# A hand-ordered two-attention kernel: paired row transfers, loads moved between queues, register loads ahead of their waits, and new weights for the planner of the step order

## The chip, the cores and the metric

The kernel runs on one core of one Trainium2 chip. The metric is the device time of one execution in microseconds (us). TensorE is called PE, VectorE DVE, ScalarE ACT, GpSimd POOL and SyncE SP. Lower is better.

## What is computed

Two transformer stages on x of shape (2, 1024, 128) in float32, each followed by a layer norm without weights:

```python
# stage 0: 8 heads of 16 features, causal, with a rank-one term per head
q, k, v = split(x @ w_qkv)
scores = q @ k.T * 0.25 + head_scales[h] * outer(q[:3] @ dirs[h], k[:3] @ dirs[h])
x = layernorm(x + softmax(causal(scores)) @ v @ w_out)
# stage 1: 16 heads of 8 features, keys and values from a latent of 64, rope
xh = rmsnorm(x); lat = layernorm(xh @ Wdkv.T) * ln_g + ln_b
q = rope(xh @ Wq.T); k = rope(lat @ Wuk.T); v = lat @ Wuv.T
x = x + softmax(causal(q @ k.T / sqrt(8))) @ v @ Wo.T
# a mixture of 4 experts, the best one alone counts for each token
e = argmax(rmsnorm(x) @ gate_w.T + gate_b)
x = layernorm(x + relu(rmsnorm(x) @ W1[e].T + b1[e]) @ W2[e].T + b2[e])
```

## The kernel before

**Groups.** Attention goes by groups of four heads of one batch: F = 0 to 3 belong to stage 0 and F = 4 to 11 to stage 1. For each group PE computes the scores once with the queries as rows, only so that DVE can take each row's maximum (steps `max`, L1370 on PE and L1887 on DVE, 20 units a group). The maxima are turned by PE (`turnmax`, L1426), split by DVE into three bf16 parts (L1747 to L1753, semaphore `np_ready`) and sent by SP into three rows of the queries' tile `qs` (step `rows`: L1094 in stage 0, L1088 in stage 1). The second pass of scores (`scores`, L1390) then subtracts them in the matmul itself; ACT takes the exponential (L1607), POOL masks the diagonal blocks (L1208), PE multiplies by the values (`pv`, L1407), ACT evacuates (L1612), PE turns and DVE divides (L1418, L1760, L1764). So a group's exponentials can't begin before its rows have landed.

**Splitting.** Queries and keys are float32 numbers split into three bf16 parts (`hi` L1632, `r1` L1901 or L1289, `mid` L1636, `lo` L1906 or L1296), in 16 blocks M of 512 tokens. Blocks 0 to 3 are batch 0 of stage 0: queries and keys of tokens 0 to 511 (M = 0, 1), then of tokens 512 to 1023 (M = 2, 3). SP stores each block to DRAM (`store`, L1076) and SP loads it again six times, once for each product of parts (`load`, L1018 in stage 0, L1010 in stage 1), into the tile of the group (`qs`, `ks`, three slots). In groups 0 to 4 each load is in two halves of 512 tokens. One exception: the keys of group 0 are loaded by POOL's queue. A load waits until its block's store has landed, and from group 3 on until the scores of the group three before are done (the slot). ACT's queue loads nothing.

**Experts.** Batch 0's tokens are sorted by expert (`places`, then eight indirect DMAs `scatter` on POOL, L1229, then `sorted` on SP), and worked on in 11 tiles: `row_turn` L1564, `row_feat`, `tile_hidden` L1574, `tile_relu` L1671, `tile_out` L1582 and L1586, `tile_sum` L1967, `tile_store` L1063, then eight indirect `collect` (L1247). Batch 1 goes densely through all experts (`hidden` L1542, `relu` L1711, `expert` L1486, `pick_up` L1981). In `tile_relu` on ACT and `tile_out` on PE the expert's number is read from SBUF into a register of the engine:

```python
pe.wait_ge(done["tile_relu"], nth("tile_relu", s, j))
wait_bank(*step)
e = pe.value_load(expert_of[0:1, j:j + 1], min_val=0, max_val=E - 1)
```

**The order.** A planner, run when the kernel is built, merges all steps into one list `SCHEDULE`. Each step has a wanted position (tables `FIRST`, `BETWEEN`, `READY`, `BY_ROWS`, `EXPERTS`, the numbers `MAX_AHEAD` and `MAX_LENGTH` for the maxima); the planner keeps model times of every engine from `COSTS` and `costs(step)`, and takes next the step whose engine would idle least, with `URGENT` as the weight of the position and `SP_IDLE`, `FEED`, `BACKLOG` as weights of idle time. Every engine, SP's queue of DMAs too, executes its steps in this order and waits on semaphores where it must. `MOST` says how many banks pairs each use of PSUM may hold.

## Time and profile before

| | us |
|---|---|
| median of 3 runs | 563.38 (559.97 to 565.47) |
| the profiled execution: its time | 565.1 |
| the profiled execution: span from first to last instruction | 563.4 |
| PE busy, PE granted clock on average | 480.2 (85%), 0.95 |
| DVE, ACT, POOL busy | 371.9 (66%), 323.6 (57%), 179.8 (32%) |

The span is the time from the first to the last instruction of the profiled execution; some 1.7 us of its time lie around it. Busy times are sums of instructions; an engine's idle time is put down to what ended it. The clock is PE's granted clock as a share of full speed (2.4 GHz); 0.50 is 1.2 GHz.

### The profile page before, as it was taken

The numbers are of one execution on the slowest core, as the hardware profiler recorded it, in microseconds if no ns is written. First come the engines' busy times: TensorE is split into PE (matmuls) and PEld (weight loads), VectorE is DVE, ScalarE is ACT, GpSimd is POOL, SyncE is SP. The second block draws the span as 40 slices with busy tenths as digits, with TensorE's granted clock in tenths as the row PEclk, the third lists the DMA queues.
The fourth block names the chain that finished last, engine by engine and source line by source line (L and its number), as shares of the span: only waits on it lengthen the run. The fifth ranks groups of instructions, "written<-read, shape, count | busy, mean of one in ns | idle before, by whom it ended". The sixth has DMA issues, their size and how long they took to land.

```text
span 563.4 us, 10237 instructions
## 1 busy us (share of the span) xinstructions
PE 480.2 (85%) x3749; PEld 223.4 (40%) x3764; DVE 371.9 (66%) x690; ACT 323.6 (57%) x488; POOL 179.8 (32%) x249
## 2 busy tenths in 40 slices
PE   5576799998899989888797998848888988999993
PEld 3242233444442333333232333312554443367762
DVE  4286977788877889688888788866356721233343
ACT  3422156576676668867685776715456677843331
POOL 9830131237554237634030222452202304601000
PEclk9977889999999999999999799976899999999998
DMA  3894030306112002012010102031000000100010
GB/s 96 214 210 132 2 96 23 94 1 243 45 56 65 25 5 83 28 52 65 17 43 9 52 3 58 6 98 45 6 12 15 8 12 20 30 1 0 20 38 20
DMA packets 31571, 28.83 MB, mean 51 GB/s; under 512 B 8017, under 2 KB 27857, under 8 KB 31250
## 3 DMA queue, kind: packets, MB, share of 16 engines
q1 hardware_dynamic: 30626, 26.34, 16.3%
q0 software_dynamic: 896, 1.84, 1.4%
q8 instruction: 31, 0.51, 0.4%
q14 instruction: 18, 0.15, 0.1%
HBM read 19.27 MB, written 9.31 MB: 51 GB/s over the span
## 4 chain that ended last, share of the span: by engine, by line
PE 58%; ACT 10%; DVE 10%; SPq 8%; issue 5%; DMA 4%; POOL 3%; ACTq 1%; another core or an unknown queue 0%; DVEq 0%; POOLq 0%
PE ps L1407 15%; PE ps L1390 10%; ACT pr L1607 7%; PE ps L1370 7%; DVE mparts L1887 6%; PE ps L1486 5%; PE ps L1542 5%; SPq L1018 4%; PE ps L1472 3%; SPq L1088 3%; DMA qs<-nparts 2%; PE ps L1466 2%; PE ps L1586 2%; PE ps L1574 2%; PE ps L1418 2%
## 5 line engine op out<-in xcount | busy, mean ns | idle before, releaser
L1887 DVE TENSOR_REDUCE mparts<-ps 128x2 f32<-128x1024 f32 (+3 forms) x240 | 260.4, 1114 | 83.0 <-PE ps L1370 78.5
L1607 ACT ACTIVATE pr<-ps 128x1024 f32<-128x1024 f32 (+1 forms) x240 | 221.2, 939 | 142.9 <-PE ps L1390 140.6
L1407 PE MATMUL ps<-pr,vs 128*32 128x512 f32 (+3 forms) x1152 | 124.4, 506 | 9.1 <-ACT pr L1607 5.7
L1390 PE MATMUL ps<-qs,ks 64*128 64x512 bf16 (+7 forms) x561 | 102.1, 339 | 21.1 <-DMA qs<-nparts 11.3
L1370 PE MATMUL ps<-ks,qs 61*128 61x512 bf16 (+7 forms) x576 | 108.7, 348 | 4.0 <-DVE mparts L1887 1.9
L1208 POOL TENSOR_SCALAR_AFFINE_SELECT pr<-pr 128x512 f32<-128x512 f32 x96 | 60.7, 635 | 156.5 <-ACT pr L1607 156.3
L1390 PEld LDWEIGHTS ps<-qs,ks 64*128 64x128 bf16 (+1 forms) x576 | 31.5, 96 | 106.7 <-issue 41.6
L1370 PEld LDWEIGHTS ps<-ks,qs 61*128 61x128 bf16 (+1 forms) x576 | 35.5, 101 | 33.3 <-ACT pr L1607 11.0
L1407 PEld LDWEIGHTS ps<-pr,vs 128*32 128x32 f32 x1152 | 23.6, 108 | 48.5 <-issue 30.1
L1711 ACT ACTIVATE work<-ps,b 128x512 f32<-128x512 f32 x32 | 21.8, 685 | 29.7 <-PE ps L1542 28.2
L1363 PE MATMUL ps<-cmask,identb 64*128 64x128 bf16 (+1 forms) x96 | 23.4, 244 | 11.8 <-DVE mparts L1887 4.8
L1486 PE MATMUL ps<-w,work 128*128 128x128 f32 x256 | 30.9, 278 | 0.0
L1486 PEld LDWEIGHTS ps<-w,work 128*128 128x128 f32 x256 | 29.3, 192 | 1.8 <-issue 1.8
L1542 PE MATMUL ps<-feat,w 128*128 128x512 f32 x64 | 29.7, 597 | 0.0
L1356 PE MATMUL ps<-cmask,identb 128*128 128x128 bf16 (+1 forms) x96 | 16.8, 260 | 8.9 <-issue 4.9
L1363 PE MATMUL ps<-cmaskx,identx 64*128 64x128 bf16 (+1 forms) x96 | 23.5, 245 | 0.0
L1981 DVE SCALAR_TENSOR_TENSOR xn<-ps,onehot,xn 128x128 f32<-128x128 f32 x24 | 6.8, 345 | 25.1 <-PE ps L1486 25.1
L1363 PEld LDWEIGHTS ps<-cmask,identb 64*128 64x128 bf16 x96 | 9.0, 94 | 36.0 <-issue 13.1
L1366 PE MATMUL ps<-cmask,identb 64*128 64x64 bf16 (+1 forms) x96 | 19.4, 202 | 0.0
L1366 PE MATMUL ps<-cmaskx,identx 64*128 64x64 bf16 (+1 forms) x96 | 19.4, 202 | 0.0
L1202 POOL COPY vs<-vall 128x256 f32<-128x256 f32 (+1 forms) x12 | 6.0, 504 | 39.8 <-PE ps L1407 39.8
L1612 ACT COPY ot<-ps 128x512 f32<-128x512 f32 x24 | 14.0, 585 | 8.1 <-PE ps L1407 8.1
(174 smaller groups left out, 563.5 us busy)
## 6 DMA issues: line engine op xcount, KB each, us to landing
qs<-scr0q SPq DMA_DIRECT2D x48, 64.0 KB, 2.4
qs<-scr1q SPq DMA_DIRECT2D x84, 32.0 KB
ks<-scr1k SPq DMA_DIRECT2D x84, 32.0 KB
ks<-scr0k SPq DMA_DIRECT2D x36, 64.0 KB, 2.3
scr0q<-parts SPq DMA_DIRECT2D x4, 384.0 KB, 3.1
scr0k<-parts SPq DMA_DIRECT2D x4, 384.0 KB, 3.6
scr1q<-parts SPq DMA_DIRECT2D x4, 384.0 KB, 2.5
scr1k<-parts SPq DMA_DIRECT2D x4, 384.0 KB, 2.7
```

Of the source, the lines that this page charges most:

```text
L1018: queue.dma_start(to, src.rearrange("(h d) t -> d h t", d=at.hd)).then_inc(k_first[half] if (F, k) == (0, 1) else qk_in[F % SLOTS][half % ...
L1208: pool.affine_select(out=p, in_=p, compare_op=ALU.is_ge, fill=0.0, base=0, pattern=[[0, HG], [1, P]], channel_multiplier=-1).then_inc(done ...
L1363: pe.matmul(bank[:, k, :, w - P:w], low[k][0][own[k], :], low[k][1][own[k], 0:nh, :], start=True, stop=False, skip_group_check=True)
L1366: pe.matmul(bank[:, k, :, w - HALF:w], high[k][0][own[k], :], high[k][1][own[k], 0:nh, HALF:P], start=False, stop=False, skip_group_check= ...
L1370: last = pe.matmul(bank[:, k, h, :], queries(F, 0, 2 * k + h0 + h, i * P, P), keys(F, 0, 2 * k + h0 + h, 512 * c, w), start=not diagonal, ...
L1390: last = pe.matmul(to[:, k, h, :], keys(F, 3, 2 * k + h0 + h, j * P, P), queries(F, 3, 2 * k + h0 + h, qb * 512 + lo, n), start=True, stop ...
L1407: last = pe.matmul(ps[VW * h:VW * (h + 1), PVB, lo:lo + n], vs[:, F % VSLOTS, j, VW * h:VW * (h + 1)], pr[:, st % PSLOTS, h, 0:n], start=( ...
L1486: last = pe.matmul(to, hid[:, e % 2, c, t * P:(t + 1) * P], w2[:, e * HC + c, :], start=False, stop=(c == HC - 1), skip_group_check=True)
L1542: pe.matmul(side(*step), w1[:, c * P:(c + 1) * P], feat[:, columns(b, i)], start=True, stop=True).then_inc(done["hidden"], 1)
L1607: act.activation(heads, scores_at(F, v), ACT.Exp, scale=GROUPS[F][0].scale).then_inc(exped, 1)
L1711: act.activation(hid[:, c // HC % 2, c % HC, :], side("hidden", b, i, c), ACT.Relu, bias=b1[:, c:c + 1]).then_inc(done["relu"], 1)
L1887: dve.tensor_reduce(heads, maxes_at(F, u), AX_X, ALU.max).then_inc(taken, 1)
```

## The change

- **rows**: in stage 1 three DMAs a group with two partitions each, where there were six with one partition each.
- **loads**: group 0's keys go from POOL's queue to SP's (`POOL_HALF = 2` is a half that group 0 doesn't have); group 1's queries and keys (24 DMAs) go from SP's queue to ACT's (`ON_ACT`).
- **splitting**: the `lo` of blocks 2 and 3, and the splitting of b2 (`b2_parts`, 4 instructions on one partition), go from DVE to POOL.
- **register loads**: in `tile_out` and `tile_relu` `value_load` stands ahead of the waits. ACT then waits for `places` ahead of the first.
- **waits added**: `scatter` t waits until scatter t-2 has landed (two semaphores in turn); `hidden` waits for its `feat`; a group's load in the planner stands behind the `rows` of the group two before.
- **planner**: new costs, positions and weights, so the order of steps changes on every engine.

```diff
-MOST = {"scores": 2, "row maxima": 2, "turns": 2, "side": 3}
+MOST = {"scores": 3, "row maxima": 2, "turns": 3, "side": 4}
-MAX_AHEAD, MAX_LENGTH = 1.2, 0.9
+MAX_AHEAD, MAX_LENGTH = 1.32, 0.72
-FIRST = [[(-2.0, -1.5), (-1.6, -1.1)], [(-0.5, 0.0), (-0.1, 0.4)]]
-BETWEEN = [[(1.2, 1.21), (2.0, 2.01)], [(3.4, 4.9), (4.1, 5.6)]]
-READY = [[(7.4, 7.9), (8.1, 8.4)], [(11.4, 11.6), (12.1, 12.2)]]
-BY_ROWS = [(8.45, 11.5)]
+FIRST = [[(-2.0, -1.5), (-1.6, -1.1)], [(-0.54, -0.04), (0.02, 0.52)]]
+BETWEEN = [[(1.12, 1.62), (1.95, 1.96)], [(3.17, 4.17), (4.41, 4.91)]]
+READY = [[(7.39, 7.79), (8.07, 8.37)], [(11.29, 11.49), (12.1, 12.2)]]
+BY_ROWS = [(8.54, 11.6)]
-EXPERTS = [[(7.9, 9.7), (9.7, 11.4)], [(11.6, 13.0), (13.0, 14.0)]]
+EXPERTS = [[(7.9, 9.7), (9.7, 11.4)], [(11.62, 12.41), (13.0, 14.0)]]
-FEED, BACKLOG = 0.2, 2.0
-SP_IDLE = 5.0
+FEED, BACKLOG = 0.22, 3.3
+SP_IDLE = 5.1
...
 # COSTS, the entries that move most
-"rows": (SP, 1.0), "x1": (POOL, 1.7), "hat0": (ACTE, 1.2), "lat_norm": (ACTE, 1.1), "tile_relu": (ACTE, 1.2), "expert": (PE, 1.15)
+"rows": (SP, 2.4), "x1": (POOL, 3.2), "hat0": (ACTE, 1.95), "lat_norm": (ACTE, 1.75), "tile_relu": (ACTE, 1.5), "expert": (PE, 0.92)
...
+def queue_of_load(F, k, half):
+    if F == 0 and k == 1:
+        return POOL if half == POOL_HALF else SP
+    return ACTE if F in ON_ACT else SP
...
-        return [(queue, 0.55 * len(PRODUCTS) if queue == POOL else 0.34 * len(PRODUCTS) * (1 + GROUPS[step[1]][0].n))]
+        return [(queue, 0.55 * len(PRODUCTS) if queue == POOL else (0.47, 0.68)[GROUPS[step[1]][0].n] * len(PRODUCTS))]
...
+LO_ON_DVE = 2
+POOL_HALF = 2
+ON_ACT = (1,)
...
-            out.append(("scores", F - SLOTS, NU - 1))
+            out += [("scores", F - SLOTS, NU - 1), ("rows", F - SLOTS + 1, 2)]
...
                     if at.n == 1:
-                        for pair_of in range(2):
-                            row = HALF * (pair_of + 1) - MAXIMA + p
-                            sp.dma_start(qs[row:row + 1, F % SLOTS, 0:2 * T],
-                                         nparts[2 * TB * pair_of:2 * TB * (pair_of + 1), place, p, :]).then_inc(rows_in, 16)
+                        row = HALF - MAXIMA + p
+                        sp.dma_start(qs[row:row + HALF + 1:HALF, F % SLOTS, 0:2 * T], nparts[0:n, place, p, :]).then_inc(rows_in, 16)
...
+                if t >= 2:
+                    pool.wait_ge(scattered[t % 2], 16 * (t // 2))
...
+                elif kind == "load" and queue_of_load(*args) == ACTE:
+                    load(act, *args)
...
+                    e = pe.value_load(expert_of[0:1, j:j + 1], min_val=0, max_val=E - 1)
                     pe.wait_ge(done["tile_relu"], nth("tile_relu", s, j))
                     wait_bank(*step)
-                    e = pe.value_load(expert_of[0:1, j:j + 1], min_val=0, max_val=E - 1)
...
+                    if j == 0:
+                        act.wait_ge(done["places"], nth("places", s))
+                    e = act.value_load(expert_of[0:1, j:j + 1], min_val=0, max_val=E - 1)
                     act.wait_ge(done["tile_hidden"], nth("tile_hidden", s, j))
                     if j >= 2:
                         act.wait_ge(done["tile_out"], nth("tile_out", s, j - 2))
-                    e = act.value_load(expert_of[0:1, j:j + 1], min_val=0, max_val=E - 1)
```

## Rows read from the trace of the kernel before

**Rows 1.** The page: busy shares, granted clock in tenths (40 slices), the chain by line.

```profile
PE 480.2 (85%) x3749; PEld 223.4 (40%) x3764; DVE 371.9 (66%) x690; ACT 323.6 (57%) x488; POOL 179.8 (32%) x249
...
PEclk9977889999999999999999799976899999999998
...
PE ps L1407 15%; PE ps L1390 10%; ACT pr L1607 7%; PE ps L1370 7%; DVE mparts L1887 6%; PE ps L1486 5%; PE ps L1542 5%; SPq L1018 4%; PE ps L1472 3%; SPq L1088 3%; DMA qs<-nparts 2%; PE ps L1466 2%; PE ps L1586 2%; PE ps L1574 2%; PE ps L1418 2%
```

**Rows 2.** Windows: length, busy time of each engine, granted clock, DMA share, GB/s.

```profile
12.90:28.00 15.10, 8.48 (x38) 4.82 (x37) 4.66 (x7) 7.56 (x15) 12.93 (x19) 0.94 0.84 204
28.00:43.90 15.90, 12.49 (x67) 7.01 (x68) 13.17 (x19) 2.88 (x5) 5.30 (x8) 0.74 0.90 203
43.90:48.70 4.80, 0.44 (x6) 0.39 (x6) 2.63 (x3) 0.00 (x0) 0.00 (x0) 0.78 0.65 206
```

**Rows 3.** Timeline of SP's queue: start, length, what, count of DMAs.

```profile
24.61 5.58 SPq L1018 DMA_DIRECT2D qs<-scr0q  x12
30.24 0.43 SPq L1076 DMA_DIRECT2D scr0k<-parts  x1
43.88 2.40 SPq L1094 DMA_DIRECT2D qs<-nparts  x3
170.01 1.80 SPq L1094 DMA_DIRECT2D qs<-nparts  x3
304.25 3.67 SPq L1088 DMA_DIRECT2D qs<-nparts  x6
370.60 4.05 SPq L1010 DMA_DIRECT2D ks<-scr1k  x12
375.23 3.14 SPq L1088 DMA_DIRECT2D qs<-nparts  x6
```

**Rows 4.** Timeline, other engines, in the start and at 373 us.

```profile
17.69 3.33 POOL L1018 DMA_DIRECT2D ks<-scr0k  x6 [0.31 <-POOL qs L1156]
18.61 0.69 DVE L1906 TENSOR_TENSOR parts<-work,parts 128x512 bf16<-128x512 f32 x1 [0.69 <-ACT parts L1636]
28.01 0.58 PE L1356 MATMUL ps<-cmask,identb 128*128 128x256 bf16 x2 [4.94 <-issue]
41.39 0.28 DVE L1753 TENSOR_TENSOR nparts<-nrow,nparts 16x128 bf16<-16x128 f32 x1
48.71 0.63 PE L1390 MATMUL ps<-qs,ks 128*128 128x512 bf16 x1 [4.37 <-DMA qs<-nparts]
373.61 0.28 DVE L1753 TENSOR_TENSOR nparts<-nrow,nparts 32x128 bf16<-32x128 f32 x1
```

**Rows 5.** The chain that ended last: the first and last of five landings of stage 1's rows.

```profile
207.28 1.79 DMA qs<-nparts
...
338.00 1.78 DMA qs<-nparts
```

**Rows 6.** Waits of PE for the rows of stage 1 (us, times), from line L1088.

```profile
  PE ps L1390: 5.6, 5
```

**Rows 7.** Windows at boundaries of groups; columns as in rows 2.

```profile
304.00:309.80 5.80, 3.29 (x36) 1.30 (x32) 4.77 (x7) 1.44 (x2) 0.43 (x1) 0.97 0.08 16
366.40:375.20 8.80, 4.66 (x59) 1.98 (x53) 5.94 (x12) 1.61 (x2) 7.25 (x9) 0.95 0.40 125
375.20:382.10 6.90, 2.69 (x14) 0.55 (x12) 5.14 (x6) 0.00 (x0) 0.28 (x1) 0.50 0.43 127
382.10:391.00 8.90, 7.89 (x52) 2.16 (x52) 5.06 (x6) 6.09 (x7) 2.53 (x4) 0.50 0.02 4
```

**Rows 8.** Waits from 395 to 472 us (us in total, times, longest).

```profile
PE ps L1582 <- ACT work L1671: 4.4, 4, 1.5
PE ps L1582 <- issue: 2.4, 5, 0.7
```

**Rows 9.** Groups by line: busy, mean ns, idle before.

```profile
L1296 POOL TENSOR_TENSOR parts<-work,parts 128x512 bf16<-128x512 f32 x12 | 13.8, 1157 | 4.1 <-ACT parts L1636 4.0
L1302 POOL TENSOR_SCALAR x<-xn,mv,rstd 128x128 f32<-128x128 f32 x16 | 12.5, 795 | 6.6 <-DVE shift L1803 6.5
```

More of the change, by code:

```diff
@@ L299, in wanted @@
         for half in halves_of_load(F):
-            add("loads", [(max(-1.05, F - 1.9) + 0.01 * half, ("load", F, k, half)) for k in range(2)])
+            add("loads", [(max(-1.05, F - LOADED_AHEAD) + 0.01 * half, ("load", F, k, half)) for k in range(2)])
     add("loads", [(F - 0.5, ("copy_v", F)) for F in range(NF)])
@@ L353 @@
-         "lat_turn": (PE, 0.58), "lat_feat": (ACTE, 0.6), "square": (ACTE, 0.62), "square_sum": (DVE, 0.7),
-         "hat": (POOL, 1.3), "x12": (POOL, 1.3), "gate": (PE, 0.95), "pick": (DVE, 2.1), "hidden": (PE, 1.0),
-         "relu": (ACTE, 0.6), "expert": (PE, 1.15), "pick_up": (DVE, 1.4), "layer_norm": (DVE, 1.4), "out": (SP, 0.5),
+         "combine": (DVE, 0.3), "rows": (SP, 2.4), "mask": (POOL, 0.64), "evac": (ACTE, 0.59), "y": (PE, 1.14),
+         "residual": (DVE, 0.7), "moments": (DVE, 1.85), "root": (DVE, 0.63), "power": (ACTE, 0.55), "hat0": (ACTE, 1.95), "x1": (POOL, 3.2),
@@ L356 @@
+         "latent": (PE, 0.97), "lat_copy": (ACTE, 0.38), "lat_moments": (DVE, 1.55), "lat_norm": (ACTE, 1.75),
+         "lat_turn": (PE, 0.58), "lat_feat": (ACTE, 0.77), "square": (ACTE, 0.62), "square_sum": (DVE, 0.7),
+         "hat": (POOL, 1.1), "x12": (POOL, 1.3), "gate": (PE, 0.95), "pick": (DVE, 2.1), "hidden": (PE, 0.88),
+         "relu": (ACTE, 0.68), "expert": (PE, 0.92), "pick_up": (DVE, 1.4), "layer_norm": (DVE, 1.4), "out": (SP, 0.5),
          "copy_v": (POOL, 0.66), "pads": (POOL, 3.6), "ones": (POOL, 4.0), "halves": (POOL, 1.7), "weights": (SP, 5.2), "moe_weights": (SP, 1.1),
@@ L380, in costs @@
     if kind == "load":
-        queue = POOL if step[1:3] == (0, 1) else SP
-        return [(queue, 0.55 * len(PRODUCTS) if queue == POOL else 0.34 * len(PRODUCTS) * (1 + GROUPS[step[1]][0].n))]
+        queue = queue_of_load(*step[1:])
+        return [(queue, 0.55 * len(PRODUCTS) if queue == POOL else (0.47, 0.68)[GROUPS[step[1]][0].n] * len(PRODUCTS))]
     if kind == "b2_parts":
-        return [(DVE, 3.0), (SP, 1.2)]
+        return [(POOL, 4.8), (SP, 1.2)]
     if kind == "r1":
@@ L387, in costs @@
     if kind == "lo":
-        return [(DVE, 0.7) if step[1] < 4 else (POOL, 1.17)]
+        return [(DVE, 0.7) if step[1] < LO_ON_DVE else (POOL, 1.17)]
     if kind == "root" and step[4] == 0:
@@ L735, in order @@
             end[step] += LANDS_LATER[kind]
-        if step[:3] == ("load", 0, 1):
-            end[step] += POOL_LANDS
+        if kind == "load" and costs(step)[0][0] != SP:
+            end[step] += POOL_LANDS if costs(step)[0][0] == POOL else AFTER_ISSUE[SP]
         if kind == "max":
@@ L895, in build @@
         order_made, rows_set = sem("order_made"), sem("rows_set")
[L896 removed]
+        scattered, collected_in = [sem(f"scattered{i}") for i in range(2)], [sem(f"collected_in{i}") for i in range(2)]
         sorted_in = [sem(f"sorted_in{p}") for p in range(-(-(TB + E - 1) // PIECES))]
@@ L936, in rows_value @@
         def rows_value(F):
-            return 48 * (F + 1) + 48 * max(0, F + 1 - ATT[0].groups)
+            return 48 * (F + 1)
         def maxima_of(F, q):
@@ L1054, in sorted_rows @@
                 j = slice(PIECES * p, min(PIECES * p + PIECES, rows_of_tiles(s)))
-                sp.wait_ge(scattered, 16 * len(tokens_of(s)))
+                for n in range(2):
+                    sp.wait_ge(scattered[n], 16 * len(tokens_of(s)) // 2)
                 if p == 0:
@@ L1099, in _ @@
                     store(*args)
-                elif kind == "load" and args[:2] != [0, 1]:
+                elif kind == "load" and queue_of_load(*args) == SP:
                     load(sp, *args)
@@ L1251, in _ @@
                 kind, *args = step
-                if kind == "load" and args[:2] == [0, 1]:
+                if kind == "b2_parts":
+                    b2_parts()
+                    continue
+                if kind == "load" and queue_of_load(*args) == POOL:
                     load(pool, *args)
```

49 lines of the change are left out of this document (24 added, 25 removed).

## The prediction

> **What bounds the kernel now.** I read the busy shares and the granted clock first, then the waits, then the chain in order of time, and last windows around the places where the chain left PE. PE is busy 480.2 of 563.4 us, no other engine is above 66% [rows 1], so most of what can be won is PE's 83 us of idle time and the time that it works below full clock. The clock stands at 0.7 to 0.8 in the slices from 28 to 70 us, and dips again near 310 and 366 us [rows 1]. Three places stand out.
>
> The first is the start. PE's first maxima of group 0 begin at 28.01 us, after 4.94 us of idle time; the first scores, which need rows, begin at 48.71, after 4.37 us in which PE waited for the rows' landing [rows 4]. Between 43.9 and 48.7 us PE is busy for 0.44 us [rows 2]. SP's queue shows why. Block 3 is split at 19.30 us (18.61 + 0.69 [rows 4]), but its store is issued at 30.24, behind twelve loads that began at 24.61 and others ahead of them [rows 3]; no key of group 0's second half can be asked for until it has landed. The first rows are ready at 41.67 (41.39 + 0.28 [rows 4]) and issued at 43.88 [rows 3], 2.2 us late, behind loads again. The 16 DMA engines are busy at 0.84 and 0.90 meanwhile [rows 2].
>
> The second is the boundary between groups of stage 1. The last part of the maxima is ready, SP issues six DMAs in 3.67 us [rows 3], the last of them lands 1.8 us later [rows 5], and only then can the scores of the group go on. The chain runs through this five times (from 204 to 334 us) [rows 5] and has 3% of the span in SP's L1088 [rows 1]; PE waits for the landing alone 5.6 us in five waits [rows 6]. The boundary at 366 to 391 us is the worst: of 15.7 us up to 382.1 PE is busy 7.35, and from 375.2 to 391 the clock is at 0.50, that is 1.2 GHz [rows 7]. There the rows are ready at 373.89 [rows 4], but SP is in a load of twelve until 374.65 (370.60 + 4.05) and issues them at 375.23 [rows 3].
>
> The third is the row of eleven expert tiles, from 395 to 472 us: PE waits 4.4 us for ACT's relu and 2.4 us for nothing that the profile shows ahead of `tile_out` (L1582), 6.8 in all [rows 8]. The 2.4 are what the register load leaves, since it stands between the wait and the first matmul.
>
> **The change, part by part.** The sum is made against the profiled execution's 565.1 us (span 563.4); the median is 563.4, so the same sum ends 1.7 lower there.
>
> Rows, six DMAs to three. Three take 1.80 us and six 3.67 [rows 3], so each boundary's rows are complete 1.87 us earlier. If all five on the chain give it whole, that is 9.4 us; if PE gives back only what it waited, 5.6 [rows 6], since between its waits PE has other work at hand (3.29 of 5.80 us busy at 304 us [rows 7]). I take 5.5, because PE is the engine near its bound. The new transfer, 32 parts onto two partitions, is not in stage 1's trace. Its landing is bounded by 1.8 us [rows 5] and by what the first rows needed under full DMA traffic: the last one was issued at about 45.7 (the end of 43.88 + 2.40 less one issue of 0.6) and the scores began at 48.71 [rows 3, 4], 3.0 us. So the gain at a boundary lies between 0.65 and 1.87 us.
>
> Here the Trainium skill speaks against the edit: DMA: Bandwidth & Descriptors, section "Why a DMA increments its semaphore by 16 and not by 1", says that the number of DMA engines is the largest up to 16 that divides the slowest dimension of both sides. By it the new destination of two partitions is carried by two engines, where the old one had sixteen. No row isolates this; if it held and cost the full 1.2 us of the bound, rows would gain 3 us in place of 5.5.
>
> The late boundary at 375 us. Its rows go in half the time (3.14 us now [rows 3]), and by 1.3 us earlier if no load stands ahead of them, which the planner's new need of `load` on `rows` and its price of 2.4 for rows favour. PE idles 8.35 us up to 382.1 and works 10.58 us at half clock from 375.2 to 391.0 (2.69 + 7.89) [rows 7], which at full clock would be half; so up to 13.6 us lie in this hole. I take 2.5, for the rows alone; the range takes 0 to 8.
>
> The start. SP loses group 1's 24 loads (24 x 0.465 = 11.2 us of issue, by 5.58 for twelve [rows 3]) and gains group 0's twelve keys (5.6 us), net 5.6 less. Group 0's keys are asked for by POOL from 17.69 to 21.02 now [rows 4]; SP is about to issue at that time too, so the first maxima start earlier only by a quicker landing: between nothing and the 4.94 us that PE idled, and I take 2. The first rows lose the 2.2 us in the queue. Block 3's store can go up to 10.9 us earlier (30.24 less 19.30), which brings the second half of group 0 forward; DVE, busy 13.17 of 15.9 us [rows 2], takes most of that back, and I count 2. Together 6, between 0 and 13 (the sum of 10.9 and 2).
>
> ACT pays for the 24 loads. It is not seen to issue one; SP's 0.465 and POOL's 0.55 (3.33 for six [rows 4]) bound the price at 11 to 13 us. ACT is busy 7.56 of 15.1 and 2.88 of 15.9 us there [rows 2], so 20 us are free, and I count nothing. If they stood in front of `hi` and `mid` of blocks 2 and 3, the stores that gate the start would be later by 2.8 us for each load of six.
>
> Register loads. `tile_out`'s wait for ACT and the register load now overlap. Of 6.8 us [rows 8] the 2.4 should go, and a little more by ACT's own load ahead of its wait (it heads the same chain, tile after tile). I take 3.5, between 0 and 6.8.
>
> Splitting on POOL. `b2_parts` is four instructions at no more than 1.16 us, the mean of L1296 [rows 9], and the two `lo` cost 1.16 in place of DVE's 0.69 [rows 4], so each is 0.5 us later on the way to the stores 2 and 3. POOL is 32% busy [rows 1] and hides b2; if it falls among diagonal masks, PE's `pv` waits up to 4.6 us once. Taken at 0 as a whole, for DVE is freed of as much. The pair-wise wait of the scatters holds POOL longer, but their data are not used until after 395 us, some 15 us later: 0.
>
> The new order. The model's prices come nearer the trace: `x1` is four instructions at 795 ns [rows 9], 3.2 us, and was priced 1.7; rows of stage 1 are 3.67 and were priced 1.0. That makes holes such as the one at 366 less likely, but the positions and weights reshuffle all twelve groups, whose effect I can't read; I take 0, with -8 to +8.
>
> Sum: 5.5 + 2.5 + 6 + 3.5 = 17.5. The profiled execution would take 547.6, the median **546**.
>
> **The rivals.** (1) *The start is bound by transfers.* With the DMA engines at 0.90 from 28 to 43.9 us [rows 2], a second queue only mixes group 1's bytes among group 0's. Then only the free tenth is won, 1.6 us in place of 6, and paired rows land late (3 in place of 5.5): 546 + 4.4 + 2.5 = 553. For it speaks the DMA share; against it that 1.5 MB of group 1 now goes ahead of block 3's keys, so the order of the bytes matters and not their sum. The Trainium skill's DMA: Bandwidth & Descriptors, section "Issuing engines are not separate DMA queues", says the same: a second issuing engine saves only issue time. By it the whole gain at the start would be the queue's.
>
> (2) *The order does more.* The corrected prices remove the hole at 366 us (up to 13.6 us, of which 2.5 are counted) and the clock's dip: 546 - 11 = 535. For it: the hole comes from rows that are late against the exponentials, and rows are what the new prices move. Against: DVE's maxima set them, not SP alone.
>
> (3) *The gains are given back.* PE is 85% busy [rows 1]; what is gained at one boundary is lost as waiting at the next, and only the register loads and a third of the start stay: 563.4 - 5.5 = 558.
>
> (4) *Slower.* The new positions make two more holes like that at 366 us. One mechanism: a group's maxima end after the exponentials of the group before, so rows, landing and an idle PE lie in series, and the clock falls to 0.50. One costs 13.6 us; two cost 27, less the 17.5: 573. It decides from the second hole on. Against it: the maxima start further ahead (1.32 groups in place of 1.2).
>
> **How the numbers follow.** The forecast has 0.40, with 540 to 551 as its own range. Rival 1 has 0.22, rival 2 0.17, rival 3 0.12 and rival 4 0.09. The range is 533 to 560: it takes in the forecast and the rivals 1 to 3, whose outer ends and rival 4 leave out about 2 in 10. A measurement of this kernel can't tell a change under 1% from none; 1% is 5.6 us, so faster means under 557.8. Faster: forecast, rivals 1 and 2 and a small part of rival 3, 0.81. Same: the rest of rival 3 and a little of the others, 0.11. Slower: 0.08.
>
> **What would show it.** In the changed profile the first scores should start near 43 us in place of 48.7, with block 3's store before 24; rows of stage 1 should be three DMAs in 1.8 us and PE's waits for them near zero; `tile_out`'s idle time should be under 4 us; ACT should show 24 DMA issues before its first exponential. If the first scores start later than 47 us, rival 1 holds. A landing of rows over 2.5 us shows the paired transfer at fault. A new stretch at clock 0.50 beside a boundary shows rival 4, and its absence after 360 us rival 2. I am wrong if the sum of PE's idle time falls by less than 10 us.

## The result, and the profile after

The changed kernel takes **522.7 us** (median of 4 runs, 519.9 to 526.2) against 563.1 in the same job; the ratio is 0.929 [0.921, 0.937]. The forecast was 546 with 533 to 560 around it: faster, as forecast, but 23 us more than forecast and outside the range. The profiled execution (519.9) is the fastest of the four, the one profiled before (565.1) is near the slowest of its kernel (565.5), so a difference between the two profiles is up to 5 us larger than the 40.3 between the medians.

The page of the changed kernel, its first three parts: busy time by engine, PE and the granted clock in 40 slices, a DMA queue that before did not have, and the chain by engine.

```profile
span 518.2 us, 10221 instructions
PE 462.2 (89%) x3749; PEld 219.3 (42%) x3764; DVE 363.7 (70%) x684; ACT 324.1 (63%) x488; POOL 179.5 (35%) x243
PE   5477899999989997998999898999989999999993
PEclk9879999999999999999999998999999999999998
q10 hardware_dynamic: 1920, 1.57, 1.8%
PE 66%; DVE 16%; ACT 10%; issue 4%; DMA 2%; SPq 1%; ACTq 0%; POOL 0%; DVEq 0%
```

The span fell by 45.2 us. Against [rows 1], PE's idle time went from 83.2 to 56.0 us (27.2 less), and its busy time from 480.2 to 462.2 for the same number of matmuls (18.0 less). The second part is the clock (480.2 times 0.950 and 462.2 times 0.983 are nearly the same, 456 and 454): from 39 us on no slice of the changed kernel is under 0.8, and the dip after 360 us is gone. Its mean is 0.983 in place of 0.950; in the other three executions of the changed kernel it is 0.970 to 0.979.

The waits of the changed kernel (engine, line, what it waited for: us in total, times, longest us); L1639, L1913 and L1420 are the exponentials, the maxima's reduction and the scores:

```profile
ACT pr L1639 <- PE ps L1420: 97.3, 137, 3.1
DVE mparts L1913 <- PE ps L1400: 39.9, 56, 8.4
PE ps L1420 <- DMA qs<-nparts: 1.7, 2, 0.9
```

The same three in the kernel before:

```profile
ACT pr L1607 <- PE ps L1390: 140.6, 136, 12.9
DVE mparts L1887 <- PE ps L1370: 78.5, 98, 6.4
PE ps L1390 <- DMA qs<-nparts: 11.3, 7, 4.4
```

The engines that PE feeds wait 82 us less, and PE hardly waits for rows.

SP's queue, timeline of the changed kernel (start, length, what, count), to be read beside [rows 3]:

```profile
23.08 0.38 SPq L1090 DMA_DIRECT2D scr0k<-parts  x1
40.81 1.89 SPq L1106 DMA_DIRECT2D qs<-nparts  x3
195.98 1.73 SPq L1101 DMA_DIRECT2D qs<-nparts  x3
```

Block 3's store went from 30.24 to 23.08. The first rows went 3.1 us earlier; stage 1's are three DMAs in about 1.7 us. The rows of the tenth group (375.23 before) are issued at 341.39, those of the last group at 404.87 in place of 456.24.

The other engines in the start of the changed kernel, timeline (idle time before and its releaser in brackets), beside [rows 4]:

```profile
20.77 0.62 ACT L1670 CAST parts<-work 128x512 bf16<-128x512 f32 x1 [4.48 <-issue]
...
27.11 0.58 ACT L1666 CAST parts<-ps 128x512 bf16<-128x512 f32 x1 [4.74 <-issue]
...
28.47 1.40 ACTq L1031 DMA_DIRECT2D ks<-scr0k  x3
...
44.64 1.02 ACT L1639 ACTIVATE pr<-ps 128x1024 f32<-128x1024 f32 x1 [3.03 <-PE ps L1420]
```
```profile
23.83 0.59 PE L1386 MATMUL ps<-cmask,identb 128*128 128x256 bf16 x2 [5.71 <-DMA ks<-scr0k]
...
44.23 0.38 PE L1420 MATMUL ps<-qs,ks 128*128 128x512 bf16 x1 [0.87 <-DMA qs<-nparts]
```

First maxima start at 23.83 (28.01 before), first scores at 44.23 (48.71). ACT issues its 24 loads between 15.12 and 29.9 us, ahead of the first exponential, and stands still twice for them (4.48 and 4.74 us with "issue" as the cause).

Windows of the changed kernel around the boundary at 341.4 us (length, busy time and instructions of PE, PEld, DVE, ACT, POOL, then granted clock, DMA share, GB/s), to be read beside [rows 7]:

```profile
325.00:341.40 16.40, 15.23 (x155) 6.21 (x149) 15.39 (x33) 12.28 (x17) 5.27 (x7) 1.00 0.01 1
341.40:350.00 8.60, 7.83 (x91) 2.95 (x89) 7.24 (x20) 6.19 (x7) 4.40 (x6) 1.00 0.28 81
350.00:368.80 18.80, 17.16 (x191) 6.18 (x195) 18.36 (x25) 13.13 (x15) 10.23 (x13) 1.00 0.24 74
```

There is no hole: PE works 7.83 of the 8.6 us behind the rows at full clock, where before it worked 7.35 of 15.7 us and then at 0.50.

The expert tiles in the changed kernel, groups by line (busy, mean ns, idle before), for `tile_out` (L1614, [rows 8]) and ACT's relu of a tile (L1707):

```profile
L1614 PE MATMUL ps<-b2p,ones 3*128 x11 | 2.5, 224 | 1.9 <-issue 1.0 <-ACT work L1707 0.9
```
```profile
L1707 ACT ACTIVATE work<-ps,b 128x128 f32<-128x128 f32 x44 | 12.5, 369 | 4.6 <-PE ps L1606 4.4
```

Before, the idle time ahead of `tile_out` was 6.9 us and ahead of ACT's relu 9.0:

```profile
L1582 PE MATMUL ps<-b2p,ones 3*128 x11 | 2.4, 222 | 6.9 <-ACT work L1671 4.4 <-issue 2.4
```

### The profile page after: what moved, and what is told of

Read it like the earlier page. It is cut to its first block, busy times and chain, and to the rows that moved or that the text cites. A ratio compares the mean times of both kernels' runs of the same rounds, so it can differ in the third digit from the quotient of the medians.

```text
span 518.2 us, 10221 instructions
## 1 busy us (share of the span) xinstructions
PE 462.2 (89%) x3749; PEld 219.3 (42%) x3764; DVE 363.7 (70%) x684; ACT 324.1 (63%) x488; POOL 179.5 (35%) x243
## 4 chain that ended last, share of the span: by engine, by line
PE 66%; DVE 16%; ACT 10%; issue 4%; DMA 2%; SPq 1%; ACTq 0%; POOL 0%; DVEq 0%
PE ps L1437 16%; DVE mparts L1913 13%; PE ps L1420 11%; PE ps L1400 8%; ACT pr L1639 7%; PE ps L1516 6%; PE ps L1574 5%; PE ps L1502 4%; PE ps L1496 4%; PE ps L1618 2%; PE ps L1606 2%; PE ps L1448 2%; PE ps L1393 2%; PE ps L1477 1%; PE ps L1386 1%
## 5 line engine op out<-in xcount | busy, mean ns | idle before, releaser
L1913 DVE TENSOR_REDUCE mparts<-ps 128x2 f32<-128x1024 f32 (+3 forms) x240 | 256.6, 1112 | 40.8 <-PE ps L1400 39.9
L1639 ACT ACTIVATE pr<-ps 128x1024 f32<-128x1024 f32 (+1 forms) x240 | 220.0, 940 | 98.5 <-PE ps L1420 97.3
L1437 PE MATMUL ps<-pr,vs 128*32 128x512 f32 (+3 forms) x1152 | 121.3, 499 | 1.2 <-ACT pr L1639 0.6
L1420 PE MATMUL ps<-qs,ks 64*128 64x512 bf16 (+7 forms) x561 | 98.0, 328 | 14.5 <-ACT pr L1639 5.0
L1400 PE MATMUL ps<-ks,qs 61*128 61x512 bf16 (+7 forms) x576 | 104.3, 333 | 7.2 <-issue 2.9
L1420 PEld LDWEIGHTS ps<-qs,ks 64*128 64x128 bf16 (+1 forms) x576 | 30.8, 95 | 88.5 <-ACT pr L1639 30.0
L1400 PEld LDWEIGHTS ps<-ks,qs 61*128 61x128 bf16 (+1 forms) x576 | 33.7, 97 | 35.9 <-DVE mparts L1913 13.1
L1326 POOL TENSOR_TENSOR parts<-work,parts 128x512 bf16<-128x512 f32 x14 | 16.2, 1156 | 20.3 <-ACT parts L1670 20.0
L1991 DVE COPY work<-ps 128x128 f32<-128x128 f32 x11 | 3.2, 290 | 23.0 <-PE ps L1618 22.8
```

What stands on the lines that cost most here:

```text
L1400: last = pe.matmul(bank[:, k, h, :], queries(F, 0, 2 * k + h0 + h, i * P, P), keys(F, 0, 2 * k + h0 + h, 512 * c, w), start=not diagonal, ...
L1420: last = pe.matmul(to[:, k, h, :], keys(F, 3, 2 * k + h0 + h, j * P, P), queries(F, 3, 2 * k + h0 + h, qb * 512 + lo, n), start=True, stop ...
L1437: last = pe.matmul(ps[VW * h:VW * (h + 1), PVB, lo:lo + n], vs[:, F % VSLOTS, j, VW * h:VW * (h + 1)], pr[:, st % PSLOTS, h, 0:n], start=( ...
L1639: act.activation(heads, scores_at(F, v), ACT.Exp, scale=GROUPS[F][0].scale).then_inc(exped, 1)
L1913: dve.tensor_reduce(heads, maxes_at(F, u), AX_X, ALU.max).then_inc(taken, 1)
```

## The experiments

Times are medians. Each ratio is against the kernel before in the same job. An effect given "by ratios" is the difference of two ratios times 563 us; by the intervals such differences are uncertain by 5 to 6 us where they are taken against the changed kernel, whose own interval is the widest, and by 3 to 4 us elsewhere.

| | kernel | us | ratio |
|---|---|---|---|
| 1 | new order, old body | 536.7 | 0.954 [0.949, 0.959] |
| 2 | old order, new body | 550.6 | 0.976 [0.971, 0.980] |
| 3 | changed, register loads behind the waits | 532.8 | 0.945 [0.941, 0.949] |
| 4 | changed, six row DMAs | 521.7 | 0.926 [0.922, 0.930] |
| 5 | changed, DVE's copy and scale replaced | 523.5 | 0.931 [0.927, 0.934] |
| 6 | before, the same replaced | 563.1 | 1.000 [0.997, 1.003] |
| 7 | changed, old banks | 526.1 | 0.935 [0.931, 0.938] |
| 8 | changed, old prices | 533.1 | 0.949 [0.945, 0.953] |
| 9 | changed, old queues | 525.0 | 0.934 [0.928, 0.939] |
| 10 | changed, old bounds on the maxima | 544.3 | 0.969 [0.962, 0.975] |
| 11 | changed, old positions | 528.6 | 0.940 [0.935, 0.945] |
| 12 | changed, all old numbers | 546.0 | 0.970 [0.965, 0.976] |
| 13 | before, new bounds | 558.5 | 0.993 [0.990, 0.996] |
| 14 | changed, `MAX_AHEAD` alone old | 534.8 | 0.951 [0.945, 0.957] |
| 15 | changed, `MAX_LENGTH` alone old | 533.4 | 0.948 [0.944, 0.953] |
| 16 | 2 with register loads behind the waits | 557.0 | 0.992 [0.989, 0.995] |
| 17 | before, new bounds, prices, banks | 551.2 | 0.978 [0.972, 0.984] |
| 18 | 2 with six row DMAs | 560.2 | 0.996 [0.992, 0.999] |

**The order or the edits? (1, 2)** The planner ahead of `build` and the body of `build` were exchanged as wholes: 1 has the new planner with the old body, 2 the reverse, with the constants that the new body asks for.

```diff
 # 2: the planner of before, and
+LO_ON_DVE = 2
+POOL_HALF = 2
+ON_ACT = (1,)
+def queue_of_load(F, k, half): ...
 # then build() of the changed kernel
```

> The order of the changed planner on the instructions of before: POOL loads group 0's keys, SP everything else, six DMAs a group for the rows, registers loaded behind the waits, b2 and four third parts on DVE, scatters without the pair-wise wait. Theory O (the order carries the gain: rows leave SP before the group ahead ends, maxima of groups lie one behind the other): about 532 us, so over 28 of the 40 us. Theory E (the edits carry what I counted, 17 us, and the order the rest): about 540. If the order needs the edits, it is above 550.

> The changed instructions (queues, paired rows, register loads, splitting on POOL, added waits) in exactly the order of steps of before. My prediction's terms without the order: 563 less 17.5, so 546. Theory O: most of these terms were waits that the order makes, so 552 to 558. Rows of group 9 stay behind group 11's load here.

The order alone takes 26.7 us away, the edits alone 12.8; their sum, 39.5, is the whole change (40.3) within its uncertainty. So two thirds come from the order, which I had taken at 0. Theory O had 532 for run 1 and 552 to 558 for run 2, theory E 540 and 546: each measured time lies between its two. In the profile of 1 PE idles 66.1 us (534.2 less 468.1) and works 468.1, against 83.2 and 480.2 before.

Where the time goes is read from ACT's exponentials (L1607, L1620 or L1639; 20 a group): the start of the first of a group's 20, in order of time, and the end of the span, all in us (differences in the text are of the unrounded times).

| group | before | 1 (order) | 2 (edits) | changed | 10 (old bounds) |
|---|---|---|---|---|---|
| first | 49.4 | 49.1 | 53.1 | 44.6 | 47.6 |
| fifth (stage 1 begins) | 209.7 | 208.0 | 212.5 | 201.4 | 212.2 |
| ninth | 340.4 | 322.0 | 338.0 | 315.6 | 331.7 |
| tenth | 382.1 | 352.5 | 376.4 | 347.2 | 367.4 |
| eleventh | 427.1 | 396.0 | 415.9 | 384.4 | 404.8 |
| end | 563.4 | 534.2 | 549.5 | 518.2 | 541.2 |

The order alone wins 1.7 us up to the fifth group, 16.8 from there to the ninth (2.8 to 6.2 a group), 11.1 at the one boundary with the hole (ninth to tenth), and nothing net behind it. Windows of the kernel before and of run 1 from the fifth group to the ninth (columns as in rows 7):

```profile
209.70:340.40 130.70, 112.27 (x1077) 42.69 (x1074) 107.38 (x166) 91.86 (x125) 45.09 (x60) 0.97 0.13 39
208.00:322.00 114.00, 103.86 (x1056) 39.06 (x1059) 103.56 (x155) 87.91 (x117) 37.27 (x50) 1.00 0.15 44
```

PE idles 10.1 us there in place of 18.4 and DVE 10.4 in place of 23.3, so both are at 91% of the stretch: the rest of the difference is the clock (1.00 for 0.97) and some work that now lies outside the stretch.

In 2 the start is worse than before, and its timelines show why (ACT first, then DVE):

```profile
18.52 2.75 ACTq L1031 DMA_DIRECT2D qs<-scr0q  x6
21.31 2.94 ACTq L1031 DMA_DIRECT2D ks<-scr0k  x6
27.43 2.75 ACTq L1031 DMA_DIRECT2D qs<-scr0q  x6
30.27 0.58 ACT L1666 CAST parts<-ps 128x512 bf16<-128x512 f32 x1 [11.14 <-issue]
```
```profile
30.89 0.69 DVE L1925 TENSOR_TENSOR work<-ps,parts 128x512 f32<-128x512 f32 x1 [12.41 <-ACT parts L1666]
```

Eighteen loads stand on ACT ahead of the `hi` of the next block. The last six go out at 27.43, in the same moment as six of SP's: both queues seem to have waited for the same landing. ACT stands still for 11.14 us, and DVE 12.41 behind it. The first rows go out at 49.32, 5.4 us later than before. In the changed kernel's order the loads are spread and ACT stands still for 4.48 and 4.74 us. By the table, 2 is 2.8 us behind the kernel before at the fifth group and 13.9 ahead at the end.

**Register loads (3, 16).**

```diff
-                    e = pe.value_load(expert_of[0:1, j:j + 1], ...)
                     pe.wait_ge(done["tile_relu"], nth("tile_relu", s, j))
                     wait_bank(*step)
+                    e = pe.value_load(expert_of[0:1, j:j + 1], ...)
 # and the same on ACT in tile_relu
```

> The changed kernel with value_load behind the waits again, order unchanged. Predicted term: 3.5 us, so 526. If PE has other work queued behind, or ACT's load is hidden, under 1 us, so 523.

> The order of before with the changed body, but with the register loads behind the waits again. The edits with them take 550.6. The load's own term, by the idle time ahead of tile_out: 3 to 4 us, 554. If the load costs in the old order what it costs in the new one: 560.

In the new order it costs 10.1 us (9.0 by ratios), in the old one 6.4 (9.2 by ratios): about twice to three times my 3.5; 16 (557.0) lies between its two numbers. The groups by line of 3, for the same two lines as above:

```profile
L1614 PE MATMUL ps<-b2p,ones 3*128 x11 | 2.4, 222 | 9.3 <-issue 6.8 <-ACT work L1707 2.6
```
```profile
L1707 ACT ACTIVATE work<-ps,b 128x128 f32<-128x128 f32 x44 | 12.5, 368 | 11.0 <-PE ps L1606 10.5 <-issue 0.4
```

PE idles 7.4 us more ahead of `tile_out` (9.3 against 1.9), and ACT 6.4 more. Where those instructions stand, in the changed kernel and then in 3 (ns min/median/max, first and last start):

```profile
L1614 PE MATMUL ps<-b2p,ones x11: 222/224/226, 374.4 to 430.0; 3*128 x11
```
```profile
L1614 PE MATMUL ps<-b2p,ones x11: 222/222/223, 381.1 to 444.4; 3*128 x11
```

The eleven tiles take 55.6 us with the loads ahead and 63.3 behind the waits: 7.7 us. The profiled run of 3 was also 4.9 us later at the rows of the fourth group (156.13 against 151.23), before any register load, so its span overstates the difference: of the 14.3 us by which it ends later, 9.4 come behind the tenth group's first exponential. Both loads were moved together, so what each costs alone isn't known. In 2 and 16 the tiles take 62.5 (394.1 to 456.6) and 67.2 us (394.4 to 461.6).

**Rows, six DMAs or three (4, 18).**

```diff
-                        row = HALF - MAXIMA + p
-                        sp.dma_start(qs[row:row + HALF + 1:HALF, ...], nparts[0:n, place, p, :])
+                        for pair_of in range(2):
+                            row = HALF * (pair_of + 1) - MAXIMA + p
+                            sp.dma_start(qs[row:row + 1, ...], nparts[2 * TB * pair_of:2 * TB * (pair_of + 1), place, p, :])
```

> The changed kernel with six DMAs of one partition for the rows of stage 1, order unchanged. Predicted term: 5.5 us, so 528. Theory O: PE waits nowhere for rows in the changed profile, since they are issued long before the scores that need them: within 1 us, 523 to 524. The landing of one and of the other form can be read here.

> The order of before with the changed body, but six DMAs for rows in place of three. The edits with three take 550.6. My term for rows was 5.5 us, what PE waits for their landing in the kernel before: 556. If rows cost nothing in this order either: 551.

In the new order six DMAs cost nothing that is resolved; 4 is within the uncertainty of the changed kernel. In the old order they cost 9.6 us (11.3 by ratios), twice my 5.5. PE's waits for the rows say both: 2 first, then 18.

```profile
PE ps L1420 <- DMA qs<-nparts: 3.1, 2, 1.7
```
```profile
PE ps L1422 <- DMA qs<-nparts: 11.8, 7, 3.5
```

Of the 11.8 us in 18, 10.4 are in stage 1, whose rows the edit changes, and in 2 only 1.4. In 4 the same wait is 1.8 us, as in the changed kernel (1.7), and none of it in stage 1. Run 1, with six DMAs in the new order, has 1.5 us in all. The transfer itself is no slower with two partitions than with one: the chains of 2 (two partitions) and of 18 (one) have these landings in stage 1, and the others of 18 take 1.75 to 2.62:

```profile
373.89 1.69 DMA qs<-nparts
```
```profile
284.20 1.75 DMA qs<-nparts
```

I had weighed a rule of the Trainium skill against this edit (DMA: Bandwidth & Descriptors, "Why a DMA increments its semaphore by 16 and not by 1"), by which two partitions are carried by two engines. No run here shows how many carried them; the landing shows no price for it.

**The queues of the loads (9).**

```diff
+def queue_built(F, k, half):
+    return POOL if (F, k) == (0, 1) else SP
 # asked by build() in place of queue_of_load; the order stays
```

> The changed kernel in its own order, but with the loads on the queues of before: GpSimd asks for group 0's keys, SyncE for group 1's queries and keys, ScalarE for none. My step 'the start' gives 6 us to the queues (2 for the first maxima, 2.2 for the first rows, 2 for block 3's store): 522.7 + 6 = 529. If transfers bind the start (my rival 1), the queues are worth 1.6: 524. If group 1's loads only fill SyncE's queue where the planner's order left it free, nothing: 523. In the trace, by the first: block 3's store after 28 us in place of 23.08, first rows issued near 43.5 in place of 40.81.

Time 525.0, 2.3 us more (2.6 by ratios), which is not resolved from nothing. SP's timeline and PE's:

```profile
30.68 0.43 SPq L1095 DMA_DIRECT2D scr0k<-parts  x1
...
45.89 1.88 SPq L1111 DMA_DIRECT2D qs<-nparts  x3
```
```profile
27.46 0.59 PE L1391 MATMUL ps<-cmask,identb 128*128 128x256 bf16 x2 [9.16 <-DMA qs<-scr0q]
...
49.09 0.59 PE L1425 MATMUL ps<-qs,ks 128*128 128x512 bf16 x2 [0.99 <-DMA qs<-nparts]
```

The queues do at the start what I said: the store is at 30.68 again, the first rows 5.1 us later, the first scores 4.9. The start varies by itself, though: run 4, with the same instructions there as the changed kernel, has its first rows at 42.09, so 3.8 to 5.1 us are the queues'. The exponentials of 9 are 5.1 us behind at the first group, 4.5 at the ninth and 3.5 at the tenth, and its profile ends 3.5 us later (521.7 against 518.2); the medians differ by less. So most of a gain at the start is handed on here, and part of it is lost at the boundary before the tenth group.

**Which part of the order? (7, 8, 10, 11, 12)** One set of numbers of the planner put back in each; in 12 all of them, the weights too.

```diff
 # 7
-MOST = {"scores": 3, "row maxima": 2, "turns": 3, "side": 4}
+MOST = {"scores": 2, "row maxima": 2, "turns": 2, "side": 3}
 # 8: COSTS, the price of a load and of an expert as before
 # 10
-MAX_AHEAD, MAX_LENGTH = 1.32, 0.72
+MAX_AHEAD, MAX_LENGTH = 1.2, 0.9
 # 11: FIRST, BETWEEN, READY, BY_ROWS, EXPERTS as before
```

> The changed kernel planned with the old MOST (scores 2, turns 2, side 3), all else new. The order changes. Theory B (a third pair of banks for scores lets PE run further ahead of ACT): 530 or more. If it is the prices that matter: 522 to 526.

> The changed kernel planned with the old prices (COSTS, load and expert), all else new: rows of stage 1 priced 1.0, x1 1.7, tile_relu 1.2, loads 2.04 and 4.08. Theory C (prices near the trace make the order): 535 or more, with holes at boundaries of groups as before. Theory B: under 527.

> The changed kernel, planned with the old bounds on how far a group's maxima may run ahead of its exponentials (MAX_AHEAD 1.2 and MAX_LENGTH 0.9 in place of 1.32 and 0.72). Theory A, the order wins because the maxima of the next group start earlier, so that no group's scores wait for rows: without it most of the order's gain beyond the prices' 10 and the banks' 3 us is lost, 522.7 + 10 or more, and rows would be issued later against the exponentials from stage 1 on. Theory B, the bounds are hardly reached and the gain lies elsewhere: 523 to 526.

> The changed kernel, planned with the old positions at which maxima, scores and experts of the later and shared groups fall due (FIRST, BETWEEN, READY, BY_ROWS, EXPERTS). Theory A, the positions carry what prices (10 us) and banks (3 us) leave of the order's 27: 535. Theory B, they only trim the start and a boundary or two: 524 to 527.

> The changed kernel, its planner with all numbers of before (prices, banks, bounds, positions, weights), so that only the new needs and queues of its steps are left of the change to the planner. By the runs so far the whole order is worth 27 us, and the edits to the kernel's body 13. If the numbers carry the order's gain, 522.7 + 24 to 27 = 547 to 550, which is the time of the edits alone (550.6). If the new needs (loads that rows wait for, loads on three queues) carry half of it: 535.

Against 522.7, the bounds cost 21.6, the prices 10.4, the positions 5.8, the banks 3.4 (not resolved), and all together 23.3. The four add up to 41 and are 23 together, so they don't simply add. Between 12 and 2, 4.6 us (3.1 by ratios, which is hardly resolved), lie the planner's new needs of the loads and its picture of the new queues. Of the expectations, 7 came out as written for the prices and 10 as its theory A, 12 is 1 us under the first of its two, 8 and 11 fall between theirs. Run 10 loses most. Its page has this clock in 40 slices, and the windows at the tenth group's rows (columns as above) are:

```profile
PEclk9877999999999997899999998995999999999998
```
```profile
345.00:363.30 18.30, 16.22 (x174) 6.21 (x174) 16.45 (x41) 11.19 (x13) 7.76 (x11) 1.00 0.03 9
363.30:372.00 8.70, 5.83 (x36) 1.68 (x38) 7.58 (x10) 3.42 (x4) 6.11 (x7) 0.53 0.36 111
```

The timelines of ACT, SP and PE in 10 at that place, in order of time:

```profile
354.97 3.77 ACT L1639 ACTIVATE pr<-ps 128x1024 f32<-128x1024 f32 x4 [0.91 <-PE ps L1420]
359.93 0.59 ACT L1646 COPY ot<-ps 128x512 f32<-128x512 f32 x1 [1.19 <-PE ps L1437]
...
363.32 1.59 SPq L1101 DMA_DIRECT2D qs<-nparts  x3
...
363.93 0.26 PE L1393 MATMUL ps<-cmask,identb 64*128 64x128 bf16 x1 [1.27 <-DVE att L1800]
...
366.70 0.61 PE L1420 MATMUL ps<-qs,ks 64*128 64x512 bf16 x2 [0.52 <-issue]
...
367.41 2.09 ACT L1639 ACTIVATE pr<-ps 128x1024 f32<-128x1024 f32 x2 [6.90 <-issue]
```

The exponentials of the group before end at 358.74, the next group's rows are only issued at 363.32, its first scores start at 366.70, and ACT has no exponential for 8.7 us (358.74 to 367.41). PE meanwhile has little but maxima, with which it can't run far ahead of DVE, and it works at 0.53 of its clock; the fall has begun behind the pause of 1.27 us at 363.93, where a matmul of this kind takes 0.26 us in place of 0.23. In the changed kernel the same rows go out while exponentials are still under way, and ACT's longest wait for scores from 325 to 366 us is 1.4 us. The slice at 0.5 is there in the clock lines of 10, 12, 14 and 15, and in none of 7, 8, 9 and 11. But this hole is the smaller part of the price. By the table, 10 is 3.0 us behind the changed kernel at the first group, 10.7 at the fifth, 16.0 at the ninth, 20.2 at the tenth and 23.0 at the end: half of it is lost before stage 1's first exponential, and 4.2 us at the boundary with the hole.

**The bounds by themselves (13, 14, 15, 17).**

```diff
 # 13, the kernel before with one line changed
-MAX_AHEAD, MAX_LENGTH = 1.2, 0.9
+MAX_AHEAD, MAX_LENGTH = 1.32, 0.72
 # 14 and 15, the changed kernel: 1.2, 0.72 and 1.32, 0.9
 # 17: 13 with the new COSTS, prices of a load and an expert, and MOST
```

> The kernel before with one line changed: MAX_AHEAD, MAX_LENGTH from 1.2, 0.9 to 1.32, 0.72, so that each group's maxima fall due earlier and closer together. Theory A, the maxima's lead is what the order wins by, whatever the other numbers: 563 - 20 = 543. Theory B, the numbers only work together (each of them put back alone brings back the same hole at 360 us, and the costs of 22, 10, 6 and 3 us add up to 41 where all together are 23): 555 or more.

> The changed kernel with MAX_AHEAD back at 1.2 and MAX_LENGTH left at 0.72: the maxima end 0.60 groups ahead of their place in place of 0.48 now (1.2 - 0.72 against 1.32 - 0.72 = 0.60), so they end later by 0.12 of a group. If the end of the maxima decides (it sets when rows are ready), about half of the 21.6 us, since both bounds back end them at 0.30: 530 to 535. If their start decides, all of it: 544.

> The changed kernel with MAX_LENGTH back at 0.9 and MAX_AHEAD left at 1.32: the maxima start as early as in the changed kernel and end 0.42 groups ahead of their place in place of 0.60. If the end decides, more than for MAX_AHEAD alone: 535 to 542. If the start decides: 523 to 526.

> The kernel before, its body untouched, planned with three of the new sets of numbers: the bounds on the maxima, the prices and the banks. The order as a whole takes this body from 563 to 537. If bounds, prices and banks work together and the rest only trims: 563 - 27 + 6 (positions) = 540 to 544. If positions or the new needs are just as necessary, so that the hole near 360 us stays: 553 or more.

Each bound alone costs 12.1 and 10.7 us (534.8 and 533.4), together 21.6. That the start of the maxima decides is out: it asked for 544 in 14 (534.8 measured) and 523 to 526 in 15 (533.4). That their end decides is not: it asked for 530 to 535 in 14, which came, and for 535 to 542 in 15, missed by 1.6 us, less than the uncertainty; whether the start counts beside it stays open. Expectation 14 has a slip: maxima with 1.2 and 0.72 end 0.48 groups ahead, with 1.32 and 0.72 they end 0.60 ahead. In the planner of before the same line wins only 0.7% (2.9 us against its own job's median, and resolved), not 20. With prices and banks it wins 2.2% (10.9 us; 551.2 lies between the two numbers of 17), against 4.6% for the whole order with the same body. So theory B of 13 holds: the numbers work together. Its remark that each of them put back alone brings back the hole doesn't: of the clock lines of 7, 8, 10 and 11 only that of 10 has the slice at 0.5. The rest, some 14 us by ratios (0.978 less 0.954), needs the positions, the weights, the new needs of the loads, or the planner's picture of the new queues and of the splitting on POOL; in the profile of 17 the rows of the tenth group are at 356.91 and those of the last at 437.83, in 1 at 346.37 and 417.20. Which of these it is was not tried in this planner.

**A collision of DVE with POOL (5, 6).** In the profile of before, DVE's scaling of a 128x8 tile takes 1.68 us, in the changed one 0.25. The first fence is before, DVE and POOL; the second is after.

```profile
4.92 1.03 DVE L1869 COPY wk<-w_qkv 128x128 f32<-128x128 f32 x1 [4.92 <-DMA sign<-in_sign]
...
6.48 1.80 POOL L1155 MEMSET ks<- 32x2048 f32 x1
6.63 1.68 DVE L1873 TENSOR_SCALAR geot<-geou 128x8 f32<-128x8 f32 x1
```
```profile
4.83 0.23 DVE L1895 COPY wk<-w_qkv 128x128 f32<-128x128 f32 x1 [4.83 <-DMA sign<-in_sign]
...
5.72 0.25 DVE L1899 TENSOR_SCALAR geot<-geou 128x8 f32<-128x8 f32 x1
```

The first store is then at 11.63 in place of 12.90. 5 and 6 replace both operations by forms with two tensors:

```diff
-            link(dve.tensor_copy(wk[:, :], w_qkv[:, C:2 * C]))
+            link(dve.tensor_tensor(wk[:, :], w_qkv[:, C:2 * C], w_qkv[:, C:2 * C], ALU.max))
-            link(dve.tensor_tensor(geou[:, :], geot[:, :], hs[:, :], ALU.mult))
-            link(dve.tensor_scalar(geot[:, :], geou[:, :], 1.0 / (3.0 * ATT[0].scale), None, ALU.mult))
+            link(dve.scalar_tensor_tensor(out=geou[:, :], in0=geot[:, :], scalar=1.0 / (3.0 * ATT[0].scale), in1=hs[:, :], ...))
```

> The changed kernel with wk's copy as a tensor_tensor (max of the same operand twice) and the one tensor_scalar folded with the product before it into a scalar_tensor_tensor, so that DVE's chain for wk holds no copy and no tensor_scalar while POOL clears tiles. In the profiles of four kernels the copy took 0.7 to 1.1 us and the tensor_scalar 1.68 us, ending with POOL's memset; in two they took 0.23 and 0.25. Theory P (DVE is held by POOL's memset): both are short in every run, the first store is at 11.6 us or earlier, and the time is that of the best runs, 520 to 522. Rival: nothing, 522 to 523, as the changed kernel mostly escapes it by itself.

> The same edit in the kernel of before. Theory P: the first store 1.3 us earlier (11.6), and 1.3 to 5 us off the time, so 558 to 562: so much of the 40 us was luck in the meeting of a DMA's landing with a memset. Rival: SP's queue of loads hides it, within 1 us of 563.

The first store of 6 is at 11.83, and its time is that of before (1.000); 5 has the time of the changed kernel. In 6 the first rows are issued at 44.02 all the same: the microsecond is swallowed by SP's queue. So in the kernel before the collision costs nothing. In the new order it is not settled, because the profile of the changed kernel, against which 5 is compared, mostly escapes it. The profiles of 3, 7, 8, 12, 14 and 15 have it (first store at 12.89 to 12.91) and their first exponential starts at 48.5 to 49.3; those of the changed kernel, 4, 5, 10 and 11 have their first store at 11.63 to 11.97 and start theirs at 44.6 to 47.6. Run 3, the same instructions as the changed kernel up to the tiles, is 4.0 us behind at its first exponential and 4.9 from the second group to the tenth. So up to some 5 us of the 45.2 between the two profiles, and of the prices read from these runs, can be this meeting; 5, which its edit frees of it, is no faster than the changed kernel (523.5 and 522.7), so in the medians it is not seen.

## Why the prediction was right or wrong

**The step that failed is "The new order. ... I take 0, with -8 to +8".** Alone it is worth -26.7 us (run 1), and -27.9 on top of the edits (550.6 to 522.7). I wrote that I couldn't read its effect, and then gave it a narrow range. Rival 2, that the order does more, had part of the mechanism: rows that are late against the exponentials, a hole at the boundary and a clock at 0.50 behind it. It priced that hole at 11 us beyond what was counted and had 0.17, and its sign, no stretch at 0.50 after 360 us, came. Run 1 bears the price out: 11.1 us from the ninth group to the tenth. What neither it nor the forecast had are the 16.8 us from the fifth group to the ninth, 2.8 to 6.2 a group, where before the clock dips only once, near 310 us. In run 1 PE's idle time falls by 17.1 us and its busy time by 12.1 in all. The waits of ACT for the scores and of DVE for the maxima, 219 us together in the kernel before, stood in the view of the waits, and I made no term for them because neither engine is the bound.

**The maxima's lead.** I used it as an argument against rival 4 (1.32 in place of 1.2) and for nothing else. Its two bounds are the part of the order that costs most when it is put back (21.6 us), though they carry little without the others (2.9 us in run 13). How a longer lead wins where there is no hole was not isolated.

**Rows: -5.5.** The mechanism was right, the size depends on the order. In the old order they are worth 9.6 to 11.3 us: I had counted the five waits of stage 1 in the kernel before, 5.6 us [rows 6], while with the changed body these waits are 10.4 us with six DMAs (run 18) and 1.4 with three (run 2). In the new order they are worth nothing that is resolved (run 4), since PE doesn't wait for stage 1's rows there whichever way they are sent. The fear of a landing up to 3 us late fell: 1.69 us in run 2.

**Register loads: -3.5, mis-sized.** They measured 6 to 10 us; the stretch of the tiles alone 7.7 us in the new order and 4.7 in the old. I took PE's 2.4 us of issue and a little more. But the load stands on ACT too, in the same chain of hidden, relu and out, and ACT's idle time grows by 6.4 us in run 3 beside PE's 7.4: it looks as if both loads come off each of eleven tiles, which no run separates. The upper bound, 6.8 us, was PE's idle time ahead of one line, and 10.1 lies above it.

**The start: -6.** What it should show came (store before 24; first scores at 44.2, not 43; 24 issues on ACT). In the new order, run 9 gives 4 to 5 us at the start and 2 to 3 in the time, which is not resolved, between the forecast and nothing. In the old order the cost for which I had allowed (2.8 us for each load of six that stands in front of `hi`) came true: ACT idles 11.1 us and the first rows are 5.4 us later. What rows and registers give there, 11.3 and 9.2 by ratios, is 20.5, and the edits as a whole are 13.6; the difference of 7 is near those 5.4, but it was not isolated. By its own sign, first scores after 47 us, rival 1 is out (44.23). But the DMA engines were busy at 0.96 from 14 to 40.8 us, above the 0.90 of before, so transfers may well bound what is left of the start; no run tests it.

**The late boundary: -2.5.** The hole is gone, but the order did it: run 2, with all the edits and the old order, still has the slice at clock 0.5, and run 1, with none of them, has not. Three DMAs in place of six didn't remove it, though 2 wins 3.2 us from the ninth group to the tenth, of which 18, with six DMAs, gives back 2.3: near the 2.5.

**Splitting and scatters: 0.** Nothing in the profiles speaks against it, and no run isolates it.

So the edits' terms (17.5) came to 12.8 measured in the old order and 14.0 in the new one, with errors in both directions that nearly cancel, which is luck, and the missing 23 us are the order's. The sign that I had set for being wrong, PE's idle time less by under 10 us, did not come: it fell by 27.2. It guards against too small a gain alone, and the miss was the other way. Rival 3, gains given back, is true of the rows in the new order and of part of the start, but the total went the other way. Rival 4 has no sign in the profile. No version beat the changed kernel by more than the uncertainty; six row DMAs (521.7) equal it.

## What to carry to other kernels

When a change re-plans the order of all steps, the order may be most of the change: don't price it by the one hole that is easy to see. What it can win is bounded by the idle time of the busiest engine and what the low clock costs it (here PE's 83.2 us and some 24 of its 480.2), of which this change took 27.2 and 18.0; where other engines wait for that engine all along (219 us here), the gain can lie all along too, and an order whose effect can't be read needs a range of that width. Where the work of one group must be complete before the next phase may start (maxima, rows, then scores), ask how far ahead of the last use it ends: a lead that is too short puts the landing and an idle engine in series, and in run 10 the work behind it ran at 0.53 of the clock. The value of an edit belongs to an order: the same three DMAs were worth 10 us in one and nothing resolved in the other, so measure each edit in the order in which it will run.

## What the runs showed of the hardware

A DVE copy (128x128) took 1.03 us beside a POOL memset and 0.23 in the changed kernel, where it began 0.09 us earlier; a scaling of 128x8 took 1.68 us and ended with POOL's memset (8.31 and 8.28), against 0.25 ahead of it, while DVE operations with two tensors took 0.17 to 0.18 us in the same stretch. The Trainium skill has the rule (SBUF — State Buffer, "Who interferes with whom": the port pair that DVE shares with GpSimd is an exclusive lock), and these rows agree.

A DMA issue that waits on ACT's queue stops ACT's computing too: ACT stood still for 11.14 us in run 2, for 18 loads whose issue alone takes 8.4 (2.75 + 2.94 + 2.75).
